# Attention scores from 32 array rows per head, in units of two heads and 1024 columns, instead of masked 128-row keys

## What is computed

```python
qkv = x @ w_qkv + b_qkv                        # x: layer-normed tokens, 4 images x 256 x 192
q, k, v = ...reshape(bsz, n, 3, H, HD)         # H = 12 heads, HD = 16
attn = softmax(einsum('bhqd,bhkd->bhqk', q, k) * HD ** -0.5)
out = einsum('bhqk,bhkd->bhqd', attn, v).reshape(bsz, n, d) @ w_proj + b_proj
```

## Time and profile before

| | us |
|---|---|
| median of three runs | 281.2 |
| the profiled execution | 279.14 |
| its span | 277.3 |
| spectral stage and first norm | 0 to 36.1 |
| prelude of the attention (to the first unit of `scores`) | 36.1 to 56.6 |
| attention loop (to the end of the last exponential) | 56.6 to 135.2 |
| last normalisation, second norm, routing | 135.2 to 174.8 |
| experts | 174.8 to 258.1 |
| end (shared expert, mixing, transposes, store) | 258.1 to 277.3 |

### The profile page before, as it was taken

The page is one execution under the profiler, slowest core; times in us unless marked ns, Lnnn a source line. Parts: engine busy times, 40 slices in busy tenths (PEclk is TensorE's granted clock), DMA queues, the critical chain, the costliest instruction groups (busy, mean ns, idle before and its releaser), DMA issues.

```text
span 277.3 us, 5843 instructions
## 1 busy us (share of the span) xinstructions
PE 249.7 (90%) x2023; PEld 188.2 (68%) x2023; DVE 185.9 (67%) x367; ACT 117.8 (42%) x218; POOL 112.7 (41%) x85
## 2 busy tenths in 40 slices
PE   3999876889999999969888869999999999999982
PEld 3989674777797797658678658455556555554871
DVE  0358699887997998873674883665666666566264
ACT  0370253244153345315523303655765576566303
POOL 8700078672085069100131043265655565653100
PEclk9999995999999999979999798999999999999998
DMA  7989993000000000172388401111111111111163
GB/s 177 248 201 284 273 345 114 0 0 4 2 0 2 0 2 0 53 218 74 111 281 262 143 2 28 28 47 57 43 57 43 53 46 57 42 45 41 40 207 115
DMA packets 24542, 25.97 MB, mean 94 GB/s; under 512 B 5767, under 2 KB 23208, under 8 KB 24520
## 3 DMA queue, kind: packets, MB, share of 16 engines
q1 hardware_dynamic: 20296, 20.30, 24.6%
q0 software_dynamic: 2400, 4.92, 6.0%
q10 hardware_dynamic: 1824, 0.47, 0.7%
HBM read 22.14 MB, written 3.54 MB: 93 GB/s over the span
## 4 chain that ended last, share of the span: by engine, by line
PE 69%; DVE 23%; ACT 2%; issue 2%; DMA 1%; POOL 1%; DVEq 0%
PE bank L1331 10%; PE bank L1359 8%; PE bank L1338 6%; PE bank L1069 5%; PE bank L1222 4%; PE bank L1070 4%; PE bank L1071 4%; DVE main L769 4%; PE bank L1122 4%; PE bank L997 4%; DVE main L758 3%; PE bank L1347 3%; PE bank L1177 3%; DVE main L730 3%; PE bank L1162 2%; PE bank L1045 2%
## 5 line engine op out<-in xcount | busy, mean ns | idle before, releaser
L286 POOL TENSOR_TENSOR rounded<-rounded,cf 128x1536 fp32r<-128x1536 f32 x12 | 38.7, 3243 | 31.0 <-ACT rounded L556 28.3
L1069 PE MATMUL bank<-rounded 128*128 128x256 f32 (+1 forms) x144 | 42.6, 296 | 4.4 <-DVE rounded L764 3.0
L604 ACT ACTIVATE main<-bank 128x512 f32<-128x512 f32 x48 | 28.7, 598 | 37.9 <-PE bank L1071 36.1
L936 DVE COPY main<-main 128x1152 f32 x43 | 33.1, 781 | 16.6 <-issue 14.8
L632 ACT ACTIVATE main<-down_all 128x576 f32 x44 | 30.0, 684 | 28.8 <-PE bank L1359 27.6
L1070 PE MATMUL bank<-rounded 128*128 128x256 f32 (+1 forms) x144 | 41.2, 286 | 0.0
L1071 PE MATMUL bank<-rounded 128*128 128x256 f32 (+1 forms) x144 | 41.1, 286 | 0.0
L758 DVE TENSOR_REDUCE main<-bank 128x2 f32<-128x512 f32 x48 | 31.0, 685 | 7.1 <-PE bank L1122 7.1
L467 POOL DMA_INDIRECT main<-xhat_rows,main x22 | 27.6, 1254 | 19.6 <-PE bank L1319 15.8
L1069 PEld LDWEIGHTS bank<-rounded 128*128 128x128 f32 x144 | 28.2, 196 | 7.7 <-DVE rounded L764 3.5
L475 POOL DMA_INDIRECT pair_rows<-main x20 | 21.7, 1083 | 26.0 <-DVE main L926 26.0
(11 more groups left out here) (164 smaller groups left out, 386.7 us busy)
## 6 DMA issues: line engine op xcount, KB each, us to landing
down_all<-wd SPq DMA_DIRECT2D x16, 288.0 KB, 4.8
main<-wg SPq DMA_DIRECT2D x16, 192.0 KB, 3.2
main<-wu SPq DMA_DIRECT2D x16, 192.0 KB, 2.9
main<-wg SPq DMA_DIRECT2D x16, 96.0 KB, 2.9
main<-wu SPq DMA_DIRECT2D x16, 96.0 KB, 3.3
main<-pair_rows SPq DMA_DIRECT2D x8, 192.0 KB, 3.7
main<-x SPq DMA_DIRECT2D x1, 768.0 KB, 8.0
xhat_rows<-main POOLq DMA_DIRECT2D x8, 96.0 KB, 3.4
```

The lines of the kernel that those rows point to most:

```text
L286: return engine.tensor_tensor(k_sb[part][:, b % 2, t], k_all[part][:, t, :].bitcast(F32).unsqueeze(1).broadcast_to([128, HPT, N]), mask.un ...
L936: vec.tensor_copy(w_gu[:, p, h, :], gu_e(expert(t, h))).then_inc(S["w_gu_ready"], 1)
L1069: mm(dst, w(0), x(0), start=first, stop=False)
```

## The change

Each head now occupies 32 rows of a tile: its 16 query channels stand twice, once as the high part and once as the low part, and its keys stand beside them with a sign such that one matmul over these 32 rows gives both products with the high key at once. A tile holds four heads (`QUAD`), an image has three such tiles (`QUADS`), and no mask is needed: a matmul takes the 32 rows of its head as its contraction rows, at row 0, 32, 64 or 96 of the array. A second matmul adds the low part of the key, and a third adds the maxima through a selecting tile `pick` and the transposed maxima `shift`. So a head's score tile still takes three matmuls, but of 32 rows each.

A unit is now two heads with all their columns: 1024 columns in two banks. There are six units an image and 24 in all instead of 48; `maxima` reduces 1024 columns an instruction, the exponential reads 1024. The units run on across images: unit n of `scores` is followed by unit n+8 (`LEAD`) of `scores_for_max`. `normalise` transposes 32 x 32 blocks, takes the reciprocal of 8 columns and transposes back, in place of the reciprocal of 256 columns and the shuffle. The projection of queries and keys goes by tiles of four heads: 12 tiles of 12 matmuls in place of 4 images of 24. The four masks an image are gone from POOL and DVE. The weights of the projection are laid out by 20 instructions on DVE (lines 704 and 709 of the new file) in place of 4, from two transfers in place of eight. Of the experts' weights 3 are loaded before the attention, 8 during it and 5 after it.

```diff
-        def one_head_keys(engine, b, part, t):
-            return engine.tensor_tensor(k_sb[part][:, b % 2, t], k_all[part][:, t, :]...broadcast_to([128, HPT, N]),
...
-        def max_bank(n):
-            return bank[2 + n % 3 if n < 12 else n % 2][:, :]
+        def max_banks(n):
+            i = 2 if n >= LEAD else 2 * ((n + 1) % 2)
+            return slice(i, i + 2)
+        def score_banks(n):
+            i = 2 * (n % 2) if n + LEAD >= B * UNITS else 0
+            return slice(i, i + 2)
...
+            for part, r, scale in ((0, 0, SCALE), (0, 1, SCALE), (1, 0, -1.0), (1, 1, 1.0), (2, 0, 1.0)):
+                for k in range(2):
+                    rows = slice(0, CH + k)
+                    vec.tensor_scalar(columns(wqkv[0], part, r)[rows, k], columns(wqkv_raw, part, r)[rows, k], scale, None, ALU.mult).then_inc(S["w_split"], 1)
...
+            def low_parts(m):
+                dve.wait_ge(S["qk_high"], m + 1)
+                vec.scalar_tensor_tensor(q_sb[:, b % 2, g], qk_bank(m)[:, 0:N], low_rows, high[:, 0, :], ALU.mult, ALU.subtract).then_inc(S["qk_split"], 1)
+                vec.tensor_tensor(k_lo[:, b % 2, g], qk_bank(m)[:, N:], high[:, 1, :], ALU.subtract).then_inc(S["qk_split"], 1)
...
             def normalise(quad):
-                vec.reciprocal(recip[:, s], bank[6 + s][:, 0:N]).then_inc(S["recip_ready"], 1)
-                vec.stream_shuffle(den[:, s], recip[:, s], [HD + i % HD for i in range(32)]).then_inc(S["den_ready"], 1)
+                vec.transpose(by_query, pv).then_inc(S["by_query_ready"], 1)
+                vec.reciprocal(recip, by_query[:, HD::32]).then_inc(S["recip_ready"], 1)
+                vec.transpose(den, recip.unsqueeze(2).broadcast_to([128, N // 32, 32])).then_inc(S["den_ready"], 1)
...
+            def project_qk(m):
+                if m >= 2:
+                    pe.wait_ge(S["qk_split"], 2 * (m - 1) if m < 6 else 2 * m)
...
+            def scores_for_max(n):
+                    pe.wait_ge(S["smax_ready"], n - 1 if n < LEAD else n)
+                for qh in range(2):
+                    for h in range(2):
+                        rows = slice(64 * pair + 32 * h, 64 * pair + 32 * h + 32)
+                        last = mm(grid[:, max_banks(n).start + h, qh * N:qh * N + N], q_sb[rows, b % 2, g, 128 * qh:128 * qh + 128],
+                                  qk_hi[rows, b % 2, g, 1, :], start=True, stop=True)
...
+            def scores(n):
+                elif n + LEAD <= B * UNITS:
+                    pe.wait_ge(S["exp_ready"], n)
+                for kh in range(2):
+                    keys = slice(128 * kh, 128 * kh + 128)
+                    for i in range(3):
+                        for h in range(2):
+                            rows = slice(64 * pair + 32 * h, 64 * pair + 32 * h + 32)
+                            w = (qk_hi[rows, b % 2, g, 1, keys], k_lo[rows, b % 2, g, keys], pick[rows, g, :])[i]
+                            x = shift[rows, b % 2, :] if i == 2 else q_sb[rows, b % 2, g, :]
+                            last = mm(grid[:, score_banks(n).start + h, kh * N:kh * N + N], w, x, start=(i == 0), stop=(i == 2))
...
+            for n in range(B * UNITS):
+                b, u = n // UNITS, n % UNITS
+                scores(n)
+                if n + LEAD < B * UNITS:
+                    scores_for_max(n + LEAD)
+                if n % 2 == 0:
+                    if 5 + n // 2 < B * QUADS:
+                        project_qk(5 + n // 2)
+                    if n:
+                        attend(n // 2 - 1)
+                if u == 4 and b + 1 < B:
+                    maxima_rows(b + 1)
+                if u == 2 and b:
+                    project_out(b - 1)
+                if u == 3 and 0 < b < B - 1:
+                    project_v(b + 1)
```

More of the change, by code:

```diff
@@ L73, in constants @@
     p = np.arange(128)
-    masks = np.stack([(p // HD == h) | (p == CH + h) for h in range(HPT)], 1) * 1.0
+    masks = np.stack([p // HD % 2 == 1, *(p % 32 == g for g in range(QUADS))], 1) * 1.0
     f = np.concatenate([
@@ L283, in program @@
         block = ctx.enter_context(nc.Block())
-        def one_head_keys(engine, b, part, t):
-            return engine.tensor_tensor(k_sb[part][:, b % 2, t], k_all[part][:, t, :].bitcast(F32).unsqueeze(1).broadcast_to([128, HPT, N]),
-                                        mask.unsqueeze(2).broadcast_to([128, HPT, N]), ALU.mult)
         def loop_pairs(engine, step):
@@ L388, in _ @@
                 sp.dma_start(dn_e(e).rearrange("p (k c) -> p k c", k=FC), a["wd"][e].rearrange("(k p) c -> p k c", k=FC)).then_inc(S["ld_experts"], 16)
[L391 to L399 removed]
+            sp.wait_ge(S["tok_ready"], B)
+            for e in range(BEFORE, E - LATE):
+                load_expert(e, S["ld_late"])
+            sp.wait_ge(S["st_done"], UNITS * B)
+            for e in range(E - LATE, E):
+                load_expert(e, S["ld_late"])
             sp.wait_ge(S["scattered"], 1)
@@ new lines, in maxima @@
+            def maxima(n):
+                b, g, pair = n // UNITS, n % UNITS // 2, n % 2
+                if n == 0:
+                    dve.wait_ge(S["bias_zeroed"], BIAS_SET)
+                dve.wait_ge(S["smax_done"], n + 1)
+                if b >= 2 and n % UNITS == 0:
+                    dve.wait_ge(S["rT_done"], b - 1)
+                col = 64 * pair + g
+                vec.tensor_reduce(negmax[:, b % 2, :, col:col + 33:32].rearrange("p q h -> p h q"),
+                                  grid[:, max_banks(n), :].rearrange("p h (q n) -> p h q n", q=2), AX.X, ALU.max, negate=True).then_inc(S["smax_ready"], 1)
```

459 lines of the change are left out of this document (212 added, 247 removed).

## The result

The changed kernel takes 295.0 us (median of four runs, 291.6 to 301.7), the kernel before 281.4 in runs beside them. The ratio is 1.044, 95% interval 1.034 to 1.054. The forecast was 274.5 with a range of 265 to 286, faster than before; the kernel is slower.

What follows compares the result with a forecast made beforehand. TensorE was taken to bound the attention loop, DVE 2 us behind. First scores at 58.9 plus a 70.3 loop gain 6.0 us, the tail 0.7: 279.14 less 6.7 is 272.4, by the median 274.5; range 265 to 286.

Steps and rivals of the forecast that it cites:

- one spell at the lower level behind the prelude: Behind the prelude, TensorE's stop of 2.7 us brings one spell at 1.2 GHz, costing 2.0 us, between 0 and 3.
- the clock falls inside the loop: Rival, 0.15: stops in every turn lower TensorE's clock in the attention loop; no gain at 0.83, 285 us at 0.77.
- signs of being wrong: Trace readings listed beforehand as refuting: loop clock under 0.9, first scores before 57 or after 61, spectral stage over 2 late.
- Pairs of 32-row matmuls overlap: In the loop's scores, two heads' small matmuls run side by side, 0.117 us a pair; TensorE saves 4.2 us an image.
- loads one behind the other: Rival, 0.11: weight loads in the loop's scores do not overlap, a pair takes 0.22 to 0.23; 286 us.
- Reduction 1.2, transposes 0.44, exponential 1.04: In the loop, us per instruction: DVE's 1024-column maxima 1.2 and 32 x 32 transposes 0.44, ACT's 1024-column exponential 1.04.
- The ring: In the loop, a cycle of waits from low parts through projection, attend, normalise and maxima to the next low parts: 6.5 us.
- plain turn: Two units of the attention loop without project_out, forecast at 6.5 us, of which TensorE works 4.4.
- the lists: The loop's instructions laid out per engine, each at the later of its engine's and semaphore's time: 66.2 us against 78.6.
- The prelude: Ahead of the loop: weight split 5.0 to 5.8 us from 16.2, norms ending near 41.6, first scores at 58.9, 2.3 later.
- The tail: Behind the last exponential, one normalisation instead of two precedes the last project_out; only 0.7 us is won.
- The late loads of the experts' weights: Behind the attention: the last five experts' loads cost nothing, as the experts start only at 174.8.

Runs made afterwards that it cites:

- The last version: Changed kernel with fills in prelude, loop and behind it, projection weights loaded earlier, GpSimd's bias addition moved, projections over all 128 rows: 272.9 us, 0.972 of the kernel before.
- the version with the clock at 1.00: Changed kernel with fills in prelude and loop, projection weights loaded earlier, GpSimd's bias addition moved, none behind the loop: 276.1 us, 0.982 of the kernel before.
- the prelude edits: In the changed kernel, projection weights and bias loaded ahead of the residual copy, GpSimd's bias addition behind DVE's norms; with fills in prelude and loop 276.1 us.

## Why the prediction was wrong

**The step that failed** is the clock's: "So I count one spell at the lower level behind the prelude: 2.0, between 0 and 3", and with it the 0.15 for the rival "the clock falls inside the loop", whose point of decision was a mean clock of 0.83. The reasoning read one quantity, how long TensorE was busy in a stretch, off. But in the changed kernel the busy time said 4.00 of 4 in stretches at 0.50. What the runs showed in its place: how many rows of the array the matmuls fill counts as well as the stops. 150 matmuls over 32 rows lost the level with no stop at all, the same over 96 and 128 rows held it, and the loop's mean clock was 0.70 (65.49 to 154.37). This was not a matter of size alone: the condition on rows is in no row of before, as its score matmuls fill 128 rows. But that busy time does not tell enough, the trace of before did show, in rows that the prediction left out (columns as in the earlier trace rows):

```profile
120.00:124.00 4.00, 3.12 (x14) 2.83 (x15) 3.32 (x5) 1.18 (x2) 0.00 (x0) 0.65 0.73 223
...
148.00:152.00 4.00, 3.15 (x24) 2.73 (x25) 1.21 (x5) 2.28 (x4) 1.07 (x2) 0.99 0.85 264
152.00:156.00 4.00, 4.00 (x13) 3.23 (x12) 3.38 (x30) 2.79 (x4) 0.00 (x0) 0.59 0.87 274
```

The level fell in more than one place of the kernel before, once behind a stretch that was busy for 3.15 of 4, where the earlier trace rows had it stay through one of 2.54.

The price that the rival had was not far off. From 135.9 us at 0.83 and 140.2 at 0.77 its own slope gives an estimate of about 146 for the last exponential at 0.70; it ended at 154.37, of which 6.6 us are the late start. Three of the prediction's signs of being wrong came true: a clock under 0.9 in 65 to 120, first scores behind 61, and a spectral stage 2.02 us late.

Where the 29.3 us between 272.4 (the forecast for a profiled run) and 301.7 lie: the loop starts 6.6 late (65.49 for 58.9), lasts 88.9 for 70.3, 18.6 more (65.49 to 154.37), the last `project_out` comes 10.5 behind the last exponential for 8.3, 2.2 more, and the rest is 1.9 longer (134.95 us of span behind it, before 133.1). Point by point:

- **Pairs of 32-row matmuls overlap**: right. 0.82 us a unit at 2.4 GHz for 0.7 to 0.8; with one row group about 1.4. The rival "loads one behind the other" is out.
- **Reduction 1.2, transposes 0.44, exponential 1.04**: right (1.22, 0.45, 1.02).
- **The ring**: right in kind, too short in sum. The last version, of 272.9 us, shows it at full clock; TensorE and then ACT of it:

```profile
57.98 0.98 PE L1163 MATMUL grid<-rounded 32*128 32x256 f32 x12
60.73 0.98 PE L1163 MATMUL grid<-rounded 32*128 32x256 f32 x12
...
67.04 0.97 PE L1163 MATMUL grid<-rounded 32*128 32x256 f32 x12
```

```profile
129.48 1.02 ACT L596 ACTIVATE main<-grid 128x1024 f32<-128x1024 f32 x1 [0.88 <-PE grid L1163]
```

  A plain turn is 6.3 us (60.73 to 67.04) where the lists had 6.5, fills included. The loop from 57.98 to 130.50 is 72.5 us. The forecast without its clock term was 68.3, so the ring and what stands in it were laid out 4.2 us too short. DVE works 4.17 us of a turn of 6.29 there (62.83 to 69.12), so it idles 2.1, not under 1.3. (TensorE's work in a turn adds to 4.3 us, where the prediction wrote 4.4; nothing hangs on it.) Turns with the image's other work are what is over: the one that holds `project_out` and V's projection took 10.2 (82.60 to 92.82) for 7.8, 0.8 of it a fill that covers no wait there; the next with `project_out` 8.6 (105.40 to 113.99) for 7.4; the last four 16.5 for 14.9.
- **The prelude**: the split ran 4.54 us for the 5.0 to 5.8 laid out, but started at 17.57, not 16.2, as the residual's transfer stood ahead of the weights in SP's queue; the spectral stage ended 2.0 us late for 1.1, inside its 0.5 to 2.4. The norm ended 0.98 us behind GpSimd's addition, where the prediction had 0.9 (39.60 to 40.5): right, and at 42.61 for 41.6 since the addition itself came later. (The Trainium skill, SBUF — State Buffer, SBUF: two separate sides, has GpSimd and DVE, in those of its modes that use two ports, share a pair of ports as an exclusive lock and not as a share of bandwidth. The trace agrees: the first of the four norms took 1.86 us, to 41.74, just behind GpSimd's end at 41.63, and each of the other three is recorded at 0.37.) From there to the first scores: 22.9 for 17.3, and 18.1 in the version with the clock at 1.00 (39.1 to 57.2). So 4.8 of the 5.6 are clock.
- **The loop's 18.6**: 88.9 less 72.5 is 16.4 us of clock (an estimate: the 72.5 holds fills, which the 88.9 does not). The prediction had counted 2.0 of clock, so 14.4 of the 18.6 are clock and 4.2 the ring.
- **The tail**: the shared expert's first matmuls took 5.33 us for 3.69 before, and the transposes ahead of them 2.92 for 1.8; the clock read 0.53 and 0.62 over 156:164. So its 2.2 are clock too. The late loads of the experts' weights cost nothing, as forecast: they were over by 167, and the experts start behind 190.

In all about 23 us are clock (4.8, 16.4 and 2.2), of which the prediction had counted 2.0. Once it is held, and with the prelude mended, the kernel takes 272.9 to 275.5, close to the 274.5 forecast. That is partly luck, since the prelude edits and a longer ring offset each other.

## What to carry to other kernels

Before cutting matmuls down to few rows of the array, ask what holds TensorE's clock. Here twelve 32-row matmuls in two row groups cost what six full ones do (0.98 us recorded for either), but the prelude and a loop of them with stops of 0.7 us each turn ran at half clock for 64 us together, and even without a stop 32-row matmuls lost the level. After any such change read the granted clock by stretches first, and where it is low, try fills of full-row matmuls into a free bank in the stops: here 112 of them took 13 us off, which only brought the kernel back to where it had been. The gain of some 2.6% needed the edits to the prelude as well.

And a busy share of 4.00 of 4 in a stretch says nothing until the clock beside it is read: an engine at half clock is busy because it is slow.

## What the runs showed of the hardware that was not expected

- 150 matmuls of 256 columns back to back: 18.2 us over 96 or 128 rows; over 32 rows over 29 us, as the level fell inside the burst (one run each).
- Matmuls in different row groups do not keep the program's order: one in rows 0 to 31 started 0.11 us ahead of earlier ones in rows 64 to 127 (82.16 and 82.27), so the description of the kernel, by which an engine does its list strictly in order, does not hold for these. Issuing head by head instead of alternating changed nothing (0.98 us recorded for twelve, both ways). A filler in rows that the work in front of it does not use did not stand where it was written; one in rows 64 to 95 left only 0.2 us of the stop.
- Once down, the level stayed so for 64 us (44 to 108) in the changed kernel, prelude and loop, and came back near 80 when fills of full rows stood in every turn.
- Four 128x192 normalisations on DVE take 1.25 us alone. Beside a GpSimd addition of 1536 columns the first of them took 1.86 us by itself, until GpSimd was done.
